# Edge tiles of 126 rows in place of 128 in a two-layer graph kernel on one core

## The reference

```
def layer0(feat, src, dst, W, b):
    m = relu(feat[src]) + 1e-7
    ex = exp(m - segment_max(m, dst)[dst])
    a = ex / segment_sum(ex, dst)[dst]
    msg = segment_sum(a * m, dst)
    return (feat + msg) @ W + b

def layer1(x, src, dst, edge_attr, Wq, bq, Wk, bk, We, be, Wv, bv):
    Q, K, V = x @ Wq + bq, x @ Wk + bk, x @ Wv + bv      # 8 heads of 12
    score = K[src] * Q[dst] / sqrt(12) * (edge_attr @ We + be)
    score = exp(clip(score.sum(-1), -5, 5))
    wV, Z = segment_sum(V[src] * score, dst), segment_sum(score, dst)
    return wV / (Z + 1e-6)

x = layernorm(x + layer0(x, src, dst, ...))
x = layernorm(x + layer1(x, src, dst, edge_attr, ...))
```

## Time and profile before

| what | value |
|---|---|
| median of 3 runs | 4863.65 us (4859.48 to 4865.23) |
| profiled execution, span from first to last instruction | 4892.4 us, 28.8 us (0.6%) over the median of the runs |
| TensorE busy | 3098.1 us (63%), 13152 matmuls |
| VectorE busy | 2300.2 us (47%) |
| ScalarE busy | 870.5 us (18%) |
| GpSimd busy | 3143.9 us (64%) |
| layer 0, first gather to start of the last | 2.9 to 2383.5 us |
| layer 1, first gather to start of the last | 2404.9 to 4877.7 us |

### The profile page before, as it was taken

The page is one execution under the profiler, slowest core; times in us unless marked ns, Lnnn a source line. Parts: engine busy times, 40 slices in busy tenths (PEclk is TensorE's granted clock), DMA queues, the critical chain, the costliest instruction groups (busy, mean ns, idle before and its releaser), DMA issues.

```text
span 4892.4 us, 43885 instructions
## 1 busy us (share of the span) xinstructions
PE 3098.1 (63%) x13152; PEld 2767.9 (57%) x13152; DVE 2300.2 (47%) x5605; ACT 870.5 (18%) x1966; POOL 3143.9 (64%) x3330
## 2 busy tenths in 40 slices
PE   3445444555555455455578777878777877877777
PEld 3344434444444444444477677767677777767676
DVE  5434344334433443344445555555555555555555
ACT  1222222222222222222201111111111111111111
POOL 6666666666666666666566666666666666666665
PEclk8666666666656667656665655565666565566665
DMA  3111111121111111111244444444444444444443
GB/s 97 40 40 43 42 39 40 40 45 40 40 44 41 39 40 45 40 39 40 67 111 111 114 112 114 112 111 117 112 111 111 114 112 114 112 114 110 115 113 98
DMA packets 290371, 383.51 MB, mean 78 GB/s; under 512 B 154382, under 2 KB 196911, under 8 KB 290127
## 3 DMA queue, kind: packets, MB, share of 16 engines
q0 software_dynamic: 132864, 251.83, 21.4%
q1 hardware_dynamic: 157263, 128.81, 9.5%
HBM read 360.62 MB, written 19.72 MB: 78 GB/s over the span
## 4 chain that ended last, share of the span: by engine, by line
POOL 31%; issue 23%; PE 18%; another core or an unknown queue 15%; DVE 9%; DMA 2%; ACT 2%; DVEq 0%; SPq 0%; ACTq 0%
POOL rows L454 31%; PE banks L605 4%; PE banks L586 4%; PE banks L577 4%; PE banks L547 3%; DVE onehot L817 2%; PE banks L596 2%; DMA rows<-in_x,src_i 1%; DVE sums L942 1%; DVE ex L930 1%; DMA rows<-key_value,src_i 1%; DVE banks L850 1%; ACT onehot_t L717 1%; DVE sums L940 1%
## 5 line engine op out<-in xcount | busy, mean ns | idle before, releaser
L454 POOL DMA_INDIRECT rows<-key_value,src_i x1661 | 1571.9, 946 | 922.2 <-issue 431.8
L454 POOL DMA_INDIRECT rows<-in_x,src_i x1661 | 1570.6, 946 | 811.6 <-issue 469.1
L547 PE MATMUL banks<-ex,onehot 128*128 128x192 f32 x3322 | 1036.0, 483 | 1026.7 <-DVE ex L930 810.5
L547 PEld LDWEIGHTS banks<-ex,onehot 128*128 128x128 f32 x3322 | 865.2, 288 | 1188.8 <-DVE ex L930 933.9
L586 PE MATMUL banks<-qw,onehot_t 128*128 128x192 f32 x1664 | 609.2, 515 | 401.2 <-ACT onehot_t L717 233.1
L605 PEld LDWEIGHTS banks<-onehot,vals 128*104 128x104 f32 x3322 | 601.2, 272 | 260.2 <-issue 210.3
L605 PE MATMUL banks<-onehot,vals 128*104 128x64 f32 x3322 | 608.2, 359 | 183.8 <-issue 151.5
L586 PEld LDWEIGHTS banks<-qw,onehot_t 128*128 128x128 f32 x1664 | 440.3, 302 | 449.1 <-ACT onehot_t L717 258.4
L577 PE MATMUL banks<-we_sb,ea 97*128 97x96 f32 x3322 | 672.1, 372 | 0.0
L577 PEld LDWEIGHTS banks<-we_sb,ea 97*128 97x128 f32 x3322 | 662.2, 295 | 0.0
L930 DVE SCALAR_TENSOR_TENSOR ex<-banks,ex 128x384 f32<-128x384 f32 x416 | 229.0, 550 | 795.7 <-issue 654.5
(11 more groups left out here) (107 smaller groups left out, 1480.4 us busy)
## 6 DMA issues: line engine op xcount, KB each, us to landing
ea<-in_edge_t SPq DMA_DIRECT2D x415, 192.0 KB
rows<-in_x,src_i POOLq DMA_INDIRECT x1661
rows<-key_value,src_i POOLq DMA_INDIRECT x1661
qw<-query SPq DMA_DIRECT2D x832, 24.0 KB
key_value<-qkv SPq DMA_DIRECT2D x24, 400.0 KB
x<-in_x SPq DMA_DIRECT2D x7, 672.0 KB, 8.2
query<-qkv SPq DMA_DIRECT2D x24, 192.0 KB
out<-outs SPq DMA_DIRECT2D x24, 192.0 KB
```

The lines of the kernel that those rows point to most:

```text
L454: pool.indirect_dma_start(out=to[0:n, r, u, :], out_offset=None, in_=table, in_offset=bass.IndirectOffsetOnAxis(ap=src_i[0:n, g * G + u:g ...
L547: last = nc.tensor.matmul(ps_sum0[b], onehot[:, r, u, :], ex[:, b, u, :], start=u == 0, stop=u == n - 1)
```

## The change

An edge tile holds `EP` = 126 edges. Node tiles keep 128. `ET` becomes 1687 and `NG` 422, and the last group has three tiles. Every tile that has edges on its partitions is cut to 126 of them, and in the edge-major free dimensions (`ea`, `onehot_t`, `ps_t`) 128 becomes 126. The last tile's gather has `TAIL_ROWS` = 64 rows instead of 32. A chunk's last group was 17 groups (`PER`) times its number; now it is the exact share of the edges, rounded up. `done_to` was made on GpSimd by one `iota` and two small fills; now VectorE fills it, one memset to a chunk.

```diff
+EP = 126
-ET = -(-EDGES // P)
+ET = -(-EDGES // EP)
-TAIL_ROWS = -(-(EDGES - (ET - 1) * P) // 32) * 32
+TAIL_ROWS = min(EP, -(-(EDGES - (ET - 1) * EP) // 32) * 32)
...
-PER = -(-(CN * EDGES) // (NODES * G * P))
...
     if c < FULL:
-        return min(PER * (c + 1) + (LAG if c < FULL - 1 else 0), NG - 1)
-    return NG - 1 if c == NC - 1 else (NT - 1) * EDGES // (NODES * G)
+        share = -(-(CN * (c + 1) * EDGES) // (NODES * G * EP))
+        return min(share + (LAG if c < FULL - 1 else 0), NG - 1)
+    return NG - 1 if c == NC - 1 else (NT - 1) * P * EDGES // (NODES * G * EP)
...
-        rows = sb("rows", [P, R1, G, KV])
-        src_i = sb("src_i", [P, NG * G], I32)
-        rel = sb("rel", [P, NG, G])
-        lane = sb("lane", [P, NG, G])
+        rows = sb("rows", [EP, R1, G, KV])
+        src_i = sb("src_i", [EP, NG * G], I32)
+        rel = sb("rel", [EP, NG, G])
+        lane = sb("lane", [EP, NG, G])
...
-        ex = sb("ex", [P, 2, G, 2 * D])
-        onehot = sb("onehot", [P, RO, G, P])
-        onehot_t = sb("onehot_t", [P, 2, 2, P])
-        ea = sb("ea", [D + 1, RE, G, P])
+        ex = sb("ex", [EP, 2, G, 2 * D])
+        onehot = sb("onehot", [EP, RO, G, P])
+        onehot_t = sb("onehot_t", [P, 2, 2, EP])
+        ea = sb("ea", [D + 1, RE, G, EP])
...
-            pool.iota(done_to[:, :], pattern=[[CN, NG // PER + 2], [0, PER]], base=-CN,
-                      channel_multiplier=0).then_inc(s_const, 1)
 
             def gather_tile(g, u, r, to, table, s):
-                n = TAIL_ROWS if g * G + u == ET - 1 else P
+                n = TAIL_ROWS if g * G + u == ET - 1 else EP
...
+            V.memset(done_to[:, 0:last_group(0) + 1], 0)
+            for c in range(FULL + 1):
+                done = V.memset(done_to[:, last_group(c) + 1:last_group(c + 1) + 1 if c < FULL else NG], min(
+                    (c + 1) * CN, (NT - 1) * P))
+            link(done)
```

More of the change, by code:

```diff
@@ L165, in build @@
         ps_sum0 = [banks[:, b, 0:W0] for b in range(2)]
-        ps_lane = [banks[:, b, W0:W0 + P] for b in range(2)]
+        ps_lane = [banks[0:EP, b, W0:W0 + P] for b in range(2)]
         ps_mt = banks[0:D, 2, :]
-        ps_relu = [banks[:, 6 + b, 0:G * D].rearrange("p (a b) -> p a b", b=D) for b in range(2)]
+        ps_relu = [banks[0:EP, 6 + b, 0:G * D].rearrange("p (a b) -> p a b", b=D) for b in range(2)]
         ps_y = banks[:, 2, 0:CT * D].rearrange("p (a b) -> p a b", b=D)
@@ L173, in build @@
         ps_misc = banks[:, 7, :]
-        ps_e = [banks[:, b, 0:G * D] for b in range(2)]
-        ps_q = [banks[:, 2 + b, 0:G * D] for b in range(2)]
-        ps_t = banks[:, 4, 0:2 * P]
+        ps_e = [banks[0:EP, b, 0:G * D] for b in range(2)]
+        ps_q = [banks[0:EP, 2 + b, 0:G * D] for b in range(2)]
+        ps_t = banks[:, 4, 0:2 * EP]
         ps_sum1 = [banks[0:W1, 5 + b, 0:WIN] for b in range(2)]
-        ps_iota = [banks[:, 5 + b, WIN:2 * WIN] for b in range(2)]
-        ps_exp = [banks[:, 5 + b, 2 * WIN:2 * WIN + G * HEADS].rearrange("p (a b) -> p a b", b=HEADS)
+        ps_iota = [banks[0:EP, 5 + b, WIN:2 * WIN] for b in range(2)]
+        ps_exp = [banks[0:EP, 5 + b, 2 * WIN:2 * WIN + G * HEADS].rearrange("p (a b) -> p a b", b=HEADS)
                   for b in range(2)]
@@ L350, in edge_by_edge @@
                             before_tile(g, k)
-                        with sp.Fori(0, P) as u:
+                        with sp.Fori(0, EP) as u:
                             src, dst = (nc.values_load_multi_w_load_instructions(
                                 e_ids[0:1, bass.ds(u + lo, 1)], engines=[SP_ENGINE], min_val=0, max_val=NT * P - 1,
-                                skip_runtime_bounds_check_because="ids are node numbers")[1][0] for lo in (0, P))
+                                skip_runtime_bounds_check_because="ids are node numbers")[1][0] for lo in (0, EP))
                             rows_of = {"src": src, "dst": dst, "edge": u}
@@ L737, in _ @@
             with act.If(irregular(act, ACT_ENGINE)):
-                with act.Fori(0, NG * G * P) as n:
+                with act.Fori(0, NG * G * EP) as n:
                     act.wait_ge(s_diff, n + 1)
@@ L748, in _ @@
                     nc.scalar.copy(prod[:, 0, 0, :], ps_e[0][:, 0:D]).then_inc(s_pcp, 1)
[L749 to L750 removed]
+                    with act.Fori(0, EP) as u:
+                        act.wait_ge(s_clip1, t * EP + u + 1)
                         nc.scalar.activation(e_prod[:, 0:HEADS], e_prod[:, 0:HEADS], ACT.Exp).then_inc(s_eexp1, 1)
@@ L790, in _ @@
             link(half)
[L791 to L796, removed]
+            V.tensor_tensor(ahead[:, :], base[:, :], done_to[:, :], ALU.subtract)
             link(V.tensor_tensor(rel[:, :, :], dst_i[:, :].rearrange("p (g k) -> p g k", k=G), first_node,
@@ L1076, in _ @@
                 scale_weights()
-                with dve.Fori(0, NG * G * P) as n:
+                with dve.Fori(0, NG * G * EP) as n:
                     dve.wait_ge(s_load, n * 32 + 32)
@@ L1147 @@
         "in_dst": dst.T,
-        "in_first": dst.reshape(NG, G * P)[:, 0].reshape(1, NG),
+        "in_first": dst.reshape(NG, G * EP)[:, 0].reshape(1, NG),
         "in_ids": np.concatenate([src, dst], axis=1),
-        "in_edge_t": edge.reshape(NG, G * P, D).transpose(0, 2, 1),
+        "in_edge_t": edge.reshape(NG, G * EP, D).transpose(0, 2, 1),
         "in_w0": np.concatenate([w0, b0[None]]),
```

59 lines of the change are left out of this document (30 added, 29 removed).

## The result

The change takes 4945.62 us (median of 4 runs, 4943.66 to 4948.29), the kernel before 4863.59 us on the same chip: a ratio of 1.0171, 95% interval 1.0157 to 1.0185, 82 us slower. The forecast was 4938 us with a range of 4895 to 5005. The time is right. What follows shows that two of its terms were not, and that their errors cancelled in these runs.

What follows compares the result with a forecast made beforehand. GpSimd's gathers were taken to pace the kernel, in groups with waits for TensorE. 76.0 - 5.6 + 1.5 + 3.0 = 74.9 us on 4863.65 gave 4938 us, range 4895 to 5005.

Steps and rivals of the forecast that it cites:

- What bounds the kernel: Whole program: GpSimd's gathers pace it; time is groups times a group's cost, four gathers at 1.25 us plus waits.
- the sign on the pace: Profile after the change: if right, gathers in a layer still follow each other at 1.43 and 1.49 us.
- 26 more gathers per layer, 76.0 us: GpSimd's queue: added gathers charged at full pace, waits included, 37.3 us in layer 0 and 38.7 in layer 1.
- The 11 us for waits in the new groups: Added gathers: the part of the 76.0 us above 65.0 us at a bare 1.25 us each, for waits on TensorE.
- Two rows fewer, -5.6 us: Each gather: 126 rows instead of 128 save 1.6 ns at 0.82 ns a row, over 3374 gathers.
- in the split of a gather: Rival on gathers: the most loaded DMA engine gets 9 rows, 13.2 ns more per gather, 4988 us; chance 0.20.
- a dearer path: Rival on gathers: uneven row counts take a slower descriptor path, each 10 ns adding 34 us; chance 0.07.
- The packets as a sign: GpSimd's queue in the profile: with 9 rows on an engine, packets per gather would be no multiple of 16.
- The waits scale with the groups, 823 us: GpSimd's idle time without issue: grows from 811.7 to 823 us; under 750 or over 900 refutes the group charge.
- The start, +1.5 us: Program start: 24 more small fills on VectorE delay ScalarE's start, going straight into GpSimd's first wait for TensorE.
- the ends, +3 us: Ends of both layers: the last group has three tiles instead of one, 1.5 us more in each.
- TensorE at nothing: TensorE's work for the six new groups charged nothing, covered by 578 us idle in layer 1; uncovered 27 us there.

Runs made afterwards that it cites:

- without late signals: Runs where GpSimd barely waits for TensorE's work, unlike those of the result: kernel before, unchanged, 4191 to 4193 us; the change, unchanged, 4433.47 us, ratio 1.0575.
- the first series: The runs of the result, with work starting up to several us after TensorE's modelled end: kernel before, unchanged, 4859 to 4865 us; the change 4944 to 4948.
- the lone program: A program of its own with only gathers of 384-byte rows, 12 per case, varying row counts and index or row tile cuts: 126 rows 976 to 980 ns.

## Why the prediction was right, point by point

**What bounds the kernel: right.** "A number of groups times a cost of a group", with GpSimd's queue as the pace, is what every experiment without late signals showed. 4192 us are 3322 gathers at 1.25 us and 40 us around them. In the first series the cost of a group stayed within 1% of what it was, 5.70 and 5.93 us for 5.74 and 5.96, as the sign on the pace (1.43 and 1.49 us) had it, and by the runs it is nearer still, since the profile of before was 0.6% long. That is why the time came out.

**26 more gathers per layer, 76.0 us: right in kind, 65 to 67 us where it could be isolated.** The change with 128-row gathers measured 67 and 65 us without late signals, within about 7 us by the intervals. The 11 us for waits in the new groups can't be checked apart.

**Two rows fewer, -5.6 us: wrong, and this is the step that failed.** I took "the line between the two sizes since 126 is right beside 128". The price doesn't go by rows but by the most loaded DMA engine, plus a toll: of the 52 ns, 13 are the ninth row, about 22 the toll, and 18 are open (below). Without late signals the term is +174 us (241 - 67), in place of -5.6. The rival "in the split of a gather" named the ninth row, at 13.2 ns, and gave 4988 us. The rule of the Trainium skill that stood there ("DMA: Bandwidth & Descriptors", "Why a DMA increments its semaphore by 16 and not by 1") is borne out by 127, 125 and 124 rows, and in the trace of the change directly: from 1000 to 1500 us GpSimd's queue moved 4928 packets of 3456 bytes, nine rows, and 704 of 36 bytes, which for 352 gathers is 14 and 2. I gave that rival 0.20. The toll I had only as "a dearer path" at 0.07, whose sign, a median above 970 ns, is the one that came true. (Its 100 ns would give 4938 + 337 = 5275 us, not 5270.)

**The packets as a sign: wrong.** I expected no multiple of 16 for 9 rows on an engine. The queue moved 134944 packets, 1686 x 80 + 64, so 80 for a gather of each layer as before: two engines without rows send a small packet instead.

**The waits scale with the groups, 823 us: wrong.** They fell to 595 us. I had written that below 750 us "my charge by the group was wrong", and so it is: a group doesn't bring a fixed amount of waiting. In the first series a group took 5.7 us in layer 0 and 5.9 us in layer 1 with and without the change, and the waits were what the gathers left of it. By the medians the late signals cost the kernel before 4863.59 - 4192.27 = 671 us and the change 4945.62 - 4433.47 = 512 us; the 159 us between them are what separates 241 from 82. That the dearer gathers themselves caused this is argued and not shown: no experiment ran under late signals. The waits mostly became rarer (219 to 175 in layer 1), and work on 126 rows, or 422 groups, could have done that as well as the gathers; the 128-row version under late signals would tell.

**The two errors against each other.** In the first series's profiles the gathers' busy time is 223 us more, issue 40 us more (940.8 less 901.0) and the waits 217 us less, which sums to 46 us of the 49 us between the spans. My sum had 49 + 16 us for the first two and 11 us more waiting. It came out right because two terms of about 200 us that I didn't have cancel. That is luck of the series of runs: without late signals the same change costs 241 us, three times the 75 of the sum.

**The start, +1.5 us, and the ends, +3 us:** ScalarE began 2.3 us later and GpSimd's first wait ended 0.7 us later; too small to be told in the time. **TensorE at nothing:** in line with the runs, since 67 and 65 us stand against 65 worked out for the gathers alone; a term of a few us would not show.

**What stays open.** In the change a gather of 126 rows takes 997 ns in two series, alone 979; the tail of 64 rows takes 915 against 901. So 18 of the 52 ns, some 60 us, have no cause yet. In whole kernels the extra goes with the cut of `rows` and `src_i`: it is there with them cut (997 ns; 933 with 112 rows, against 926 alone; tails of 911 to 917) and missing with them whole (945 ns, tails of 899 and 903 in the 128-row version; 979 in the kernel before with 126 rows). But in the lone program the same cut costs nothing (978 and 901 ns), so the shapes by themselves don't explain it. Why TensorE's signals were late in one series of four, and whether the chip or something else decides it, is open too.

## What to carry to other kernels

Choose the number of rows of an indirect gather by how it divides over the 16 DMA engines: a multiple of 16, and as near 128 as the data allow (128 rows 944 ns, 126 rows 979, 127 rows 2540). By an estimate from 863 ns for 2 rows on an engine and 13.1 ns a row, about 840 ns of a gather are fixed, and 0.30 us of issue come on top, so fewer and fuller gathers win over smaller ones. And when an engine shows regular waits, reckon with their taking up what you add or remove before the time moves: this change cost 82 us beside 812 us of such waits and 241 us without them.

## What the runs showed of the hardware that I had not expected

- Indirect gather of n rows, time on GpSimd: 863 ns (32), 900 (64), 911 (96), 926 (112), 944 (128), 979 (120), 979 (126), 1192 (125), 1282 (124), 2540 (127).
- Two rows less than 128 cost 34 to 52 ns more; a row more on the most loaded engine costs 13.1 ns.
- The same program took 4864 us in one series and 4191 to 4193 us in three others on three chips, with the same gathers; the 701 us between the two profiles are idle time of GpSimd before its gathers, mostly put down to TensorE or to no known engine.
- Near the start one gather takes far longer than the rest, 3.23 us (at 11.86 us) before and 4.70 us (at 16.04 us) in the change, while VectorE works on the indices. No run shows why.
